# Cross-attention of a decoder layer: the layer-norm root, the output projection and the router's small DVE work put in other places

## The chip, the cores and the metric

The kernel runs on one core of one Trainium2 chip. The metric is the device time of one execution in microseconds; the median of 3 runs of the kernel before is 1839.6 us (1839.06 to 1843.44). TensorE is called PE, VectorE DVE, ScalarE ACT, GpSimd POOL, SyncE SP.

## The reference, cut to what matters

One pre-norm decoder layer on x of shape (8, 224, 512) with a context of (8, 750, 512): self-attention, cross-attention with distance biases, and a mixture of 8 experts of which each token takes 2.

```python
x = x + attn(_layernorm(x))
# cross-attention: 16 heads of 32, 224 queries and 750 keys for each of 8 batches
scores = einsum('bhqd,bhkd->bhqk', q, k) * scale + bias    # bias = -slope[h] * |key - query - (750 - 224)|
out    = einsum('bhqk,bhkd->bhqd', softmax(scores), v) @ Wo + bo
x = x + out
h = _layernorm(x)                                          # (x - m) / sqrt(v + eps)
# router of the mixture
scores = h @ Wr.T + br                                     # 8 experts
idx = top_k(scores + biases_N, 2); val = softmax(scores)[idx]; val = val / val.sum()
# the expert: silu(a) * b, down projection, weighted sum, all in fp32
```

fp32 products are made of high and low parts that are rounded for PE: `w_hi`, `w_lo`, and three matmuls for one product.

## The kernel before, in words

The program is a chain of phases. The change lies in `cross_phase`, which takes from about 720 to 1215 us of the profiled execution. It walks through 32 steps, one for each batch and group of four heads (`GROUPS` = 4 groups make a batch), with a loop over s from -1 to 31. In iteration s, for each of the four heads hh:

- PE makes the transposed scores of step s + 1 (`second_scores`, three banks `a_st_bank`, line 1719) and the plain scores of step s + 2 (`first_scores`, three banks `a_s_bank`, line 1700). The plain scores serve the row maxima alone.
- DVE reduces each plain bank to maxima (`maxima`, line 1959) and so sets it free. PE can be ahead of DVE by the three banks and no more.
- ACT takes the exponential of each transposed bank (`exp`, line 1865) and sets it free.
- POOL adds the exponentials of step s + 1 in pairs (`sums`, lines 1568 and 1572): two additions for each head until step 25, and one after that.

After the four heads PE does `values(s)`: 24 matmuls a head group of probabilities by V (line 1748), the transposition of the row maxima of step s + 2 (`turn_max`, line 1734), and the sums over the keys (line 1758). DVE does `row_maxima(s + 2)` (line 1965), for which `turn_max` waits, and then `normalise(s - 1)`: a reciprocal (line 1972) and a product (line 1976). ACT copies the turned maxima into the query tile (`query_rows`, line 1857), for which the next transposed scores wait. POOL splits the normalised output into high and low part (`split_o`, lines 1579 and 1581), behind its sums.

The order is written out by hand: each engine has its own loop with the same indices, and `note` lists in which order banks are taken. Once every four iterations a batch is finished, and work is inserted between the heads. For batch b:

- iteration 4b + 5: `project_out` (line 1771 to 1773), 12 matmuls for each half of the queries, after heads 1 and 3; it waits for `split_o` of step 4b + 3. DVE adds the residual (line 1985), and at the iteration's end takes the `moments` (lines 1990, 1993). POOL adds the output bias to the next batch's rows (line 1558).
- iteration 4b + 6: ACT takes the root of the variance (`root`, line 1876) before head 1. The square root and the exponential need different function tables, and each change is an ACT_TABLE_LOAD. DVE then makes the normalised rows (`hidden`, lines 1997, 2000), PE turns them after head 3. POOL fetches rows (line 1554).
- iteration 4b + 7: PE makes the router's scores (`route`, line 1812) after head 0.

The router's small DVE work, each instruction waiting for the one before it by `then`: `choose` (top two of two batches, at the end of iterations 11, 19 and 27), `slots` (places of the chosen rows, at the end of 20 and 28), `weights` (at the end of 24 and 29). At iteration 3 ACT makes four `w_hi` (line 1902) and DVE four `w_lo` (line 2090), all ahead of head 0. `GOES` says at which iterations PE makes the ranks (`ranks`) that `slots` reads.

## Time and profile before

| | |
|---|---|
| median of 3 runs | 1839.6 us |
| profiled execution | 1850.8 us, its span 1849.1 us |
| PE busy | 1702.0 us (92%) |
| DVE busy | 1069.2 us (58%) |
| ACT busy | 746.2 us (40%) |
| POOL busy | 757.9 us (41%) |
| mean granted PE clock | 0.962 of full speed |

The profiled execution is 11.2 us above the median. The span is the time from the first to the last instruction. Busy shares are means over phases with different limits. In a timeline, a row gives the start, the duration, the engine, the line, what is written and read, and in brackets how long the engine was idle before, and who released it. Rows of PE overlap, since matmuls are pipelined.

### The profile page before, as it was taken

How to read it: one execution, taken by the hardware profiler on the slowest of the kernel's cores; microseconds unless marked ns; L12 is line 12 of the kernel's file. 1: busy time of each engine (PE TensorE's matmuls, PEld its weight loads, DVE VectorE, ACT ScalarE, POOL GpSimd, SP SyncE). 2: the span in 40 equal slices, each digit the busy share in tenths (PEclk: the TensorE clock that was granted, in tenths of full speed). 3: DMA queues.
4: the chain of work that ended last, by engine and by line, in shares of the span. 5: the costliest groups of instructions: out<-in, count | busy, mean ns of one | idle time of the engine just before them, and what ended most of it. 6: DMA issues, size and time to landing. Idle time of an engine off the chain costs nothing. (4 is left out here: it accounts for less than half of the span.)

```text
span 1849.1 us, 34693 instructions
## 1 busy us (share of the span) xinstructions
PE 1702.0 (92%) x11064; PEld 1367.4 (74%) x11064; DVE 1069.2 (58%) x1893; ACT 746.2 (40%) x1332; POOL 757.9 (41%) x856
## 2 busy tenths in 40 slices
PE   6997999999999987899899898889999999999997
PEld 5885777777777766677777676667778787887775
DVE  5553455555555545777777877574563545436553
ACT  3223343433343333655565555522442424224441
POOL 3000322323322322888778657432451515115541
PEclk9998999999999997899899999879999999999999
DMA  7736566655665745997778677244663737355763
GB/s 227 228 131 174 160 174 177 180 167 167 176 178 157 203 133 129 187 197 162 165 154 173 133 153 183 67 129 123 216 223 114 224 114 232 103 144 192 245 218 91
DMA packets 211744, 309.77 MB, mean 168 GB/s; under 512 B 21728, under 2 KB 151344, under 8 KB 207136
## 3 DMA queue, kind: packets, MB, share of 16 engines
q1 hardware_dynamic: 186656, 223.90, 45.5%
q0 software_dynamic: 15472, 41.14, 10.2%
q10 hardware_dynamic: 9504, 43.26, 6.2%
q8 instruction: 68, 1.11, 0.3%
q14 instruction: 44, 0.36, 0.1%
HBM read 224.56 MB, written 83.66 MB: 167 GB/s over the span
## 5 line engine op out<-in xcount | busy, mean ns | idle before, releaser
L1959 DVE TENSOR_REDUCE a_part_max<-a_s_bank 112x1 f32<-112x500 f32 (+1 forms) x384 | 234.8, 672 | 64.3 <-PE a_s_bank L1700 53.5
L1865 ACT ACTIVATE a_prob<-a_st_bank 125x448 f32<-125x448 f32 x384 | 194.5, 545 | 94.6 <-PE a_st_bank L1719 74.8
L2578 DVE TENSOR_TENSOR e_u_sb<-e_u_bank,e_b_row 128x512 f32<-128x512 f32 x134 | 92.2, 688 | 226.6 <-PE e_u_bank L2343 215.9
L2341 PE MATMUL e_u_bank<-e_w_hi,e_xT_hi 128*128 128x512 f32 x536 | 214.6, 400 | 1.2 <-DVE e_w_lo L2571 0.4
L2343 PE MATMUL e_u_bank<-e_w_hi,e_xT_lo 128*128 128x512 f32 x536 | 211.2, 394 | 0.0
L2342 PE MATMUL e_u_bank<-e_w_lo,e_xT_hi 128*128 128x512 f32 x536 | 210.7, 393 | 0.0
L2501 POOL DMA_INDIRECT out<-l_rows,e_y_row x33 | 53.0, 1605 | 316.6 <-ACT l_rows L2455 163.1
L2402 ACT ACTIVATE e_g_hi<-e_g_bank 128x256 fp32r<-128x256 f32 x133 | 51.2, 385 | 313.2 <-PE e_g_bank L2350 299.0
L1568 POOL TENSOR_TENSOR a_part_sum<-a_prob 125x448 f32<-125x448 f32 x128 | 146.4, 1147 | 66.3 <-ACT a_prob L1865 66.1
L876 POOL TENSOR_TENSOR m_prob_sum<-m_prob 112x224 f32<-112x224 f32 x128 | 85.3, 672 | 170.7 <-ACT m_prob L1084 170.2
L2341 PEld LDWEIGHTS e_u_bank<-e_w_hi,e_xT_hi 128*128 128x128 f32 x536 | 101.8, 190 | 25.4 <-DVE e_xT_lo L2566 3.9
L1572 POOL TENSOR_TENSOR a_part_sum<-a_part_sum,a_prob 125x448 f32<-125x448 f32 x100 | 114.5, 1145 | 14.4
L2343 PEld LDWEIGHTS e_u_bank<-e_w_hi,e_xT_lo 128*128 128x128 f32 x536 | 101.6, 190 | 22.1
L2342 PEld LDWEIGHTS e_u_bank<-e_w_lo,e_xT_hi 128*128 128x128 f32 x536 | 101.8, 190 | 20.6
L2360 PE MATMUL e_y_bank<-e_w_hi,e_g_hi 128*128 128x512 f32 x264 | 115.0, 435 | 0.5 <-POOLq L2508 0.5
L2477 POOL TENSOR_TENSOR e_w_lo<-e_w_raw,e_w_hi 128x1024 fp32r<-128x1024 f32 x28 | 100.8, 3611 | 28.3 <-ACT e_w_hi L2412 28.3
L2361 PE MATMUL e_y_bank<-e_w_lo,e_g_hi 128*128 128x512 f32 x264 | 104.5, 396 | 0.0
L2362 PE MATMUL e_y_bank<-e_w_hi,e_g_lo 128*128 128x512 f32 x264 | 103.9, 394 | 0.0
L1153 DVE SCALAR_TENSOR_TENSOR m_kt_lo<-m_o_bank,m_b_col,m_kt_hi 128x500 fp32r<-128x500 f32 x48 | 35.5, 739 | 106.3 <-ACT m_kt_hi L1093 100.9
L2584 DVE TENSOR_TENSOR e_g_sb<-e_gate,e_u_sb 128x256 f32<-128x256 f32 x134 | 65.2, 487 | 42.5 <-ACT e_gate L2397 32.1
L1084 ACT ACTIVATE m_prob<-m_st_bank 112x448 f32<-112x448 f32 x128 | 67.6, 541 | 51.6 <-PE m_st_bank L1011 51.3
L1167 DVE TENSOR_REDUCE m_row_max<-m_s_bank 112x2 f32<-112x448 f32 x128 | 79.0, 617 | 10.7 <-PE m_s_bank L998 10.7
(388 smaller groups left out, 4381.7 us busy)
## 6 DMA issues: line engine op xcount, KB each, us to landing
e_w_raw<-L_ffn_Wl SPq DMA_DIRECT2D x96, 512.0 KB, 8.0
e_b_row<-L_ffn_bl ACTq DMA_DIRECT2D x33, 1024.0 KB, 6.0
k<-m_kt_hi SPq DMA_DIRECT2D x48, 250.0 KB, 3.2
k<-m_kt_lo SPq DMA_DIRECT2D x48, 250.0 KB, 4.2
m_c_in<-ctx POOLq DMA_DIRECT2D x12, 896.0 KB, 9.6
m_q_st<-q SPq DMA_DIRECT2D x96, 112.0 KB, 3.0
m_k_st<-k SPq DMA_DIRECT2D x96, 112.0 KB, 3.0
v<-m_cv SPq DMA_DIRECT2D x48, 224.0 KB
```

Of the source, the lines that this page charges most:

```text
L1568: pool.tensor_tensor(part_sum[w][:, hh, :, :], prob[w][:, hh, 0:2, :], prob[w][:, hh, 2:4, :], ALU.add).then_inc(sum_done, 1)
L1572: pool.tensor_tensor(part_sum[w][:, hh, :, :], part_sum[w][:, hh, :, :], prob[w][:, hh, 4:6, :], ALU.add).then_inc(sum_done, 1)
L1865: act.activation(prob[s % 2][:, hh, 2 * u:2 * u + 2, :], st_bank[n % SB][0:CR, 0:2 * S].rearrange("p (e q) -> p e q", e=2), ACT.Exp).then_ ...
L1959: dve.tensor_reduce(out, scores, AX.X, ALU.max).then_inc(s_free, 1)
L2341: pe.matmul(out, xT_hi[:, slot, k, :], w_h, start=(k == 0), stop=False)
L2342: pe.matmul(out, xT_hi[:, slot, k, :], w_l, start=False, stop=False)
L2343: last = pe.matmul(out, xT_lo[:, slot, k, :], w_h, start=False, stop=(k == KT - 1))
L2360: pe.matmul(y_bank[slot][:, :], g_hi[:, q % 2, t, :], w2_hi[:, q, t, :], start=first, stop=False)
L2361: pe.matmul(y_bank[slot][:, :], g_hi[:, q % 2, t, :], w2_lo[:, q, t, :], start=False, stop=False)
L2362: last = pe.matmul(y_bank[slot][:, :], g_lo[:, q % 2, t, :], w2_hi[:, q, t, :], start=False, stop=end)
L2477: pool.tensor_tensor(w2_lo[:, q, :, :], w2_raw[:, q, :, :], as_f32(w2_hi[:, q, :, :]), ALU.subtract).then_inc(w2_ready, 1)
L2578: dve.tensor_tensor(u_sb[:, q % 2, :, :], u_bank[q % 2][:, :].rearrange("p (h n) -> p h n", h=2), b1_row[:, slot, :, HC * q:HC * q + HC], ...
```

## The change

1. **Root.** ACT's `root(b)` moves from before head 1 of iteration 4b + 6 to the end of iteration 4b + 5, ahead of `query_rows`. `moments(b)` moves from the end of iteration 4b + 5 to behind its second residual, ahead of head 3's maxima.
2. **Projection.** `project_out` and `residual` come after heads 0 and 2 in place of 1 and 3.
3. **Choices.** `choose` for batches 0 to 3 moves from the ends of iterations 11 and 19 to 13 and 21, in two parts, after heads 0 and 2 (where PE projects). The one at the end of 27 stays.
4. **Places and weights.** The first ranks move from iteration 20 to 21, `slots` is cut in four (after head 3 of 21 and 22, after heads 1 and 3 of 23), `weights` in three (after head 3 of 24, heads 0 and 1 of 25). The second ranks come after head 1 of 28 in place of head 3, with the parts of `slots` after heads 1, 2, 3 and at the end of 28, and those of `weights` after heads 1, 2, 3 of 29. ACT's exponentials of the router go to before head 1 of 24 and before head 0 of 29.
5. **Weight splits.** At iteration 3 one `w_hi` and one `w_lo` stand ahead of each head.

No arithmetic is added or taken away.

```diff
-    GOES = {20: (0, 8), 28: (8, FIRST_TILES)}
+    GOES = {21: (0, 8), 28: (8, FIRST_TILES)}
+    RANKED = {21: 3, 28: 1}
...
-                        if hh % 2 == 1 and batch_at(s, 1) is not None:
+                        if hh % 2 == 0 and batch_at(s, 1) is not None:
                             project_out(batch_at(s, 1), hh // 2)
...
-                        if s in GOES and hh == 3:
+                        if s in GOES and hh == RANKED[s]:
                             ranks(s)
...
-                        if s == 3 and hh == 0:
-                            act.wait_ge(dlo_ready, HEADS // 2)
-                            act.wait_ge(w_loaded, DMA)
-                            for kk in range(KT):
-                                act.activation(w_hi[:, kk, :], w_raw[:, kk, :], ACT.Copy).then_inc(whi_ready, 1)
-                        if hh == 1 and batch_at(s, 2) is not None:
-                            root(batch_at(s, 2))
+                        if s == 3:
+                            if hh == 0:
+                                act.wait_ge(dlo_ready, HEADS // 2)
+                                act.wait_ge(w_loaded, DMA)
+                            act.activation(w_hi[:, hh, :], w_raw[:, hh, :], ACT.Copy).then_inc(whi_ready, 1)
+                        if s == 24 and hh == 1:
+                            score_exp(21)
+                        if s == 29 and hh == 0:
+                            score_exp(28)
...
+                    if batch_at(s, 1) is not None:
+                        root(batch_at(s, 1))
                     if s + 2 < STEPS:
                         query_rows(s + 2)
...
+                        if s in (13, 21) and hh % 2 == 0:
+                            choose((s - 13) // 4, (s - 13) // 4 + 2, hh // 2)
+                        if (s, hh) == (24, 3):
+                            weights(21, 0)
...
+                        if s == 29 and hh:
+                            weights(28, hh - 1)
+                        if hh % 2 == 0 and batch_at(s, 1) is not None:
                             residual(batch_at(s, 1), hh // 2)
+                            if hh == 2:
+                                moments(batch_at(s, 1))
...
+                        if (s, hh) == (21, 3):
+                            slots(21, 0)
...
+                        if s == 28 and hh:
+                            slots(28, hh - 1)
```

ACT in iterations 5 and 6, before (`third` and `a_q_st` are query tiles, `a_std` is the root):

```order
L1857 ACTIVATE third<-a_st_bank 8x896
L1865 ACTIVATE a_prob<-a_st_bank 125x448 x12
L1857 ACTIVATE a_q_st<-a_st_bank 8x896
L1865 ACTIVATE a_prob<-a_st_bank 125x448 x3
L1876 ACT_TABLE_LOAD
L1876 ACTIVATE a_std<-a_mv,a_eps 112x2
L1865 ACT_TABLE_LOAD
L1865 ACTIVATE a_prob<-a_st_bank 125x448 x9
```

And the same place of the changed kernel:

```order
L1858 ACTIVATE third<-a_st_bank 8x896
L1866 ACTIVATE a_prob<-a_st_bank 125x448 x12
L1877 ACT_TABLE_LOAD
L1877 ACTIVATE a_std<-a_mv,a_eps 112x2
L1858 ACTIVATE a_q_st<-a_st_bank 8x896
L1866 ACT_TABLE_LOAD
L1866 ACTIVATE a_prob<-a_st_bank 125x448 x12
```

The root and both table loads now stand around `query_rows` and no longer between exponentials.

PE at the first projection half of iteration 5, before: heads 0 and 1 (their last rows) and the first three of twelve projection matmuls.

```order
L1700 MATMUL a_s_bank<-a_k_st,a_q_st 112x250 x2
L1704 MATMUL a_s_bank<-a_rel_q,a_d_hi 112x224
L1719 MATMUL a_st_bank<-third 125x224 x2
L1700 MATMUL a_s_bank<-a_k_st,a_q_st 112x500
L1719 MATMUL a_st_bank<-third 125x224 x2
L1700 MATMUL a_s_bank<-a_k_st,a_q_st 112x500
L1719 MATMUL a_st_bank<-third 125x224 x2
L1723 MATMUL a_st_bank<-a_rel_k,a_d_hi 125x224
L1700 MATMUL a_s_bank<-a_k_st,a_q_st 112x250 x2
L1704 MATMUL a_s_bank<-a_rel_q,a_d_hi 112x224
L1771 MATMUL a_s_bank<-a_w_hi,a_o_split 112x512
L1772 MATMUL a_s_bank<-a_w_lo,a_o_split 112x512
```

And now, from the end of head 0:

```order
L1701 MATMUL a_s_bank<-a_k_st,a_q_st 112x250 x2
L1705 MATMUL a_s_bank<-a_rel_q,a_d_hi 112x224
L1772 MATMUL a_s_bank<-a_w_hi,a_o_split 112x512
L1773 MATMUL a_s_bank<-a_w_lo,a_o_split 112x512
L1774 MATMUL a_s_bank<-a_w_hi,a_o_split 112x512
```

PE reaches the reading of `a_o_split`, which POOL writes, one head sooner.

DVE at the second half of iteration 13, now (in the order before, the four rows from CAST to `r_before` stood at the end of iteration 11, ahead of head 0, and the BN rows behind the product `a_o_f`):

```order
L2024 CAST a_top_f<-a_top_i 112x32
L2026 TENSOR_TENSOR r_pick<-a_iota_e,a_top_f 112x32 x2
L2028 TENSOR_TENSOR r_mask<-r_pick 112x32
L2030 TENSOR_TENSOR r_before<-r_before,r_mask 112x8 x4
L1992 TENSOR_TENSOR a_x_new<-a_s_bank,a_xh 112x512
L1997 BN_STATS a_bn<-a_x_new 112x6 x2
L2000 BN_AGGR a_mv<-a_bn 112x2 x2
L1966 TENSOR_REDUCE a_part_max<-a_s_bank 112x1 x2
L1966 TENSOR_REDUCE a_part_max<-a_s_bank 112x2
L1972 TENSOR_REDUCE a_row_max<-a_part_max 112x4x2
L1979 RECIPROCAL a_rinv<-a_or_bank 128x224
L1983 TENSOR_TENSOR a_o_f<-a_or_bank,a_rinv 128x224
```

Ahead of the row maxima and of `a_o_f` there now stand the moments, and in 13 and 21 the second part of the choice.

## Rows read from the trace of the kernel before

**Rows 1.** Page, section 1: PE; busy us, share of the span, instructions.

```profile
PE 1702.0 (92%) x11064; PEld 1367.4 (74%) x11064; DVE 1069.2 (58%) x1893; ACT 746.2 (40%) x1332; POOL 757.9 (41%) x856
```

**Rows 2.** Windows between turned maxima: PE, PEld, DVE, ACT, POOL busy; PEclk, DMA, GB/s.

```profile
776.64:1168.33 391.69, 359.89 (x3524) 283.00 (x3520) 303.04 (x576) 214.17 (x386) 284.27 (x279) 0.95 0.75 161
776.64:792.77 16.13, 14.06 (x121) 11.22 (x118) 12.79 (x20) 9.19 (x17) 12.90 (x13) 0.79 1.08 195
...
846.69:857.17 10.48, 10.38 (x120) 8.22 (x116) 9.14 (x16) 7.04 (x13) 9.28 (x11) 1.00 0.88 184
857.17:873.47 16.30, 16.20 (x145) 12.30 (x141) 10.95 (x19) 7.04 (x13) 12.13 (x12) 1.00 0.54 107
...
888.63:900.62 11.99, 11.89 (x136) 9.72 (x133) 8.68 (x15) 7.03 (x13) 9.22 (x10) 1.00 0.82 177
900.62:916.93 16.31, 12.94 (x120) 10.43 (x116) 14.41 (x37) 7.23 (x13) 11.34 (x12) 0.79 0.57 115
...
988.63:1002.25 13.62, 11.32 (x128) 8.95 (x124) 12.30 (x23) 10.57 (x18) 11.30 (x11) 1.00 1.04 232
...
1118.70:1168.33 49.63, 44.98 (x446) 34.18 (x442) 34.87 (x85) 20.57 (x39) 28.84 (x31) 0.97 0.50 135
1168.33:1189.79 21.46, 16.84 (x173) 12.72 (x169) 8.14 (x20) 15.99 (x22) 16.30 (x17) 0.84 0.44 135
```

**Rows 3.** PE's waits from 776.64 to 1189.79: total us, times, longest.

```profile
PE a_st_bank L1719 <- ACT a_prob L1865: 18.4, 10, 2.9
PE a_s_bank L1700 <- DVE a_part_max L1959: 12.8, 8, 3.3
```

**Rows 4.** Timeline of iteration 6 at the root.

```profile
823.05 1.28 ACT L1876 ACT_TABLE_LOAD   x1
...
824.66 1.28 ACT L1865 ACT_TABLE_LOAD   x1
...
826.55 0.48 PE L1719 MATMUL a_st_bank<-a_q_st,a_k_st 104*125 104x224 f32 x2 [2.20 <-ACT a_prob L1865]
```

**Rows 5.** Timeline, tail and head of iteration 5; DVE at its end.

```profile
803.26 0.35 PE L1734 MATMUL a_st_bank<-ident,a_row_max 112*8 112x112 f32 x2
...
806.26 0.27 PE L1704 MATMUL a_s_bank<-a_rel_q,a_d_hi 112*112 112x224 f32 x1
...
817.11 2.48 PE L1748 MATMUL a_or_bank<-a_prob,a_v_sb 125*32 125x224 f32 x48
817.22 0.69 DVE L1985 TENSOR_TENSOR a_x_new<-a_s_bank,a_xh 112x512 f32<-112x512 f32 x1 [1.93 <-PE a_s_bank L1773]
...
819.79 1.28 DVE L1990 BATCH_NORM_STATS2 a_bn<-a_x_new 112x6 f32<-112x512 f32 x2
```

**Rows 6.** Timeline of POOL: ends of two steps in a row, and the bias.

```profile
848.52 0.67 POOL L1581 TENSOR_TENSOR a_o_split<-a_o_f,a_o_split 128x224 fp32r<-128x224 f32 x1
...
859.75 0.67 POOL L1581 TENSOR_TENSOR a_o_split<-a_o_f,a_o_split 128x224 fp32r<-128x224 f32 x1
...
874.96 2.38 POOL L1558 TENSOR_TENSOR a_xh<-a_xh,a_out_bias 112x1024 f32<-112x1024 f32 x1
```

**Rows 7.** Timeline of the choice at the end of iteration 11, and a later one.

```profile
901.35 0.74 DVE L2014 TENSOR_TENSOR a_zb<-r_z,a_c_bias 112x32 f32<-112x32 f32 x1
...
903.22 0.18 DVE L2021 CAST a_top_f<-a_top_i 112x32 f32<-112x32 uint32 x1
...
903.76 1.09 DVE L2025 TENSOR_TENSOR r_mask<-r_pick 112x32 f32<-112x32 f32 x1
...
906.64 3.02 DVE L1959 TENSOR_REDUCE a_part_max<-a_s_bank 112x1 f32<-112x500 f32 x5
907.38 0.76 PE L1700 MATMUL a_s_bank<-third 100*112 100x500 f32 x1 [3.27 <-DVE a_part_max L1959]
...
1135.16 0.19 DVE L2025 TENSOR_TENSOR r_mask<-r_pick 112x32 f32<-112x32 f32 x1
```

**Rows 8.** Timeline of DVE: the weight splits of iteration 3.

```profile
778.70 3.01 DVE L2090 TENSOR_TENSOR a_w_lo<-l_rows,a_w_hi 128x512 fp32r<-128x512 f32 x4 [1.52 <-ACT a_w_hi L1902]
```

More of the change, by code:

```diff
@@ L2006, in scores_done, with choose, best @@
                                       r_bias[:, :].unsqueeze(1).broadcast_to([QR, 2, EXPERTS]), ALU.add).then_inc(s_free, 1)
-                def choose(b0, b1):
+                def choose(b0, b1, part=None):
                     t0, n = 2 * b0, 2 * (b1 - b0)
+                    tiles = slice(t0, t0 + n)
+                    TE = [QR, n, EXPERTS]
+                    if part in (None, 0):
+                        best(t0, n, b1)
+                    if part == 0:
+                        return
+                    then(dve.tensor_copy(top_f[:, 0:n, :], top_i[:, 0:n, :]))
+                    for j in range(2):
+                        last = dve.tensor_tensor(pick[j][:, tiles, :], iota_e[:, 0:n, :], top_f[:, 0:n, j].unsqueeze(2).broadcast_to(TE), ALU.is_equal)
+                    then(last)
+                    then(dve.tensor_tensor(mask[:, tiles, :], pick[0][:, tiles, :], pick[1][:, tiles, :], ALU.add))
+                    for t in range(t0, t0 + n):
+                        then(dve.tensor_tensor(before[:, t + 1, :], before[:, t, :], mask[:, t, :], ALU.add))
+                    dve.sem_inc(chosen, 1)
+                def best(t0, n, b1):
                     tiles = slice(t0, t0 + n)
@@ L2020, in choose, with slots @@
                     then(last)
-                    then(dve.tensor_copy(top_f[:, 0:n, :], top_i[:, 0:n, :]))
-                    for j in range(2):
-                        last = dve.tensor_tensor(pick[j][:, tiles, :], iota_e[:, 0:n, :], top_f[:, 0:n, j].unsqueeze(2).broadcast_to(TE), ALU.is_equal)
-                    then(last)
-                    then(dve.tensor_tensor(mask[:, tiles, :], pick[0][:, tiles, :], pick[1][:, tiles, :], ALU.add))
-                    for t in range(t0, t0 + n):
-                        then(dve.tensor_tensor(before[:, t + 1, :], before[:, t, :], mask[:, t, :], ALU.add))
-                    dve.sem_inc(chosen, 1)
-                def slots(s):
+                def slots(s, part):
                     t0, t1 = GOES[s]
@@ L2041, in slots @@
-                    dve.tensor_tensor(row[:, 0:n, :], bank[0:QR, 0:n * EXPERTS].rearrange("p (t e) -> p t e", e=EXPERTS),
-                                      places["first_slot"][:, :].unsqueeze(1).broadcast_to(TE), ALU.add).then_inc(s_free, 1)
-                    dve.wait_ge(s_free, at + 1)
-                    for j in range(2):
-                        then(dve.tensor_tensor(prod[:, 0:n, :], row[:, 0:n, :], pick[j][:, t0:t1, :], ALU.mult))
-                        then(dve.tensor_reduce(slot_f[:, j, 0:n], prod[:, 0:n, :], AX.X, ALU.add))
@@ L2060, in weights @@
+                def weights(s, part):
                     t0, t1 = GOES[s]
```

117 lines of the change are left out of this document (65 added, 52 removed).

## The prediction, written before the changed kernel was run

> **What bounds the kernel now.** I read the busy times first: PE is busy for 92% of the span [rows 1], so only what PE waits for, and the clock it runs at, can be won. Then I cut the phase that changes into iterations, from one turned maximum to the next [rows 2]. Without anything odd there are four kinds, and a batch takes one of each: a plain iteration takes 10.48 us (846.69:857.17), one with the projection 16.30, one with the turning of the hidden rows 13.62 less a wait of 2.20, so 11.4, and one with the router's scores 11.99. In the first, second and fourth the granted clock is 1.00 and PE is busy for all but 0.1 us. Iterations 3 to 29 are 8 plain ones (3 counted so), 7, 6 and 6: 83.8 + 114.1 + 68.5 + 71.9 = 338.3 us. They take 391.7 [rows 2]. The excess of 53.4 us is what this change can reach, and 2.9 us or a bit more in iteration 30.
>
> The excess is of two sorts. PE's waits [rows 3]: 18.4 us on the exponentials, of which 2.9 lie in iteration 30, and 12.8 on DVE's maxima, 28.3 in the window. And the clock: 0.95 over the window, 5% of 391.7 = 19.6 us. Together 48; the rest is small stretching. After some waits PE runs at 1.2 GHz for a while: iteration 12 waits 3.27 us [rows 7] and is 5.8 us over plain at a clock of 0.79; iteration 18 waits 2.2 us, its clock stays 1.00, and it loses no more than the wait [rows 2].
>
> **The root.** In iteration 6 ACT loads a table (1.28 us), takes the root, loads the other (1.28 us), and PE stands for 2.20 us [rows 4], since exponentials do not free their banks. There are seven such roots, six in the window and one in iteration 30. Moved to the end of iteration 4b + 5, the root lies beside `values`. Count from P, the end of the second projection half (817.11, rows 5). PE does head 3, about 1.66 us (plain iteration 10.48, less 3.1 to the end of head 0 and 2.4 for the values part, over three heads), then 2.4 us of values (817.11 to 819.52, rows 2 and 5), and turns the maxima at T = P + 4.1. ACT's last exponential ends near P + 2.2, the load and the root at P + 3.8, so `query_rows`, which waits for T, is not held. The second load ends at about T + 2.6 and the first exponential at T + 3.15, where PE wants its bank at T + 3.1. I take 0.2 us of wait in each: 1.2 us left in six iterations instead of 13.2.
>
> The page on ScalarE in the Trainium skill (ScalarE: Activation LUTs, What ACT_TABLE_LOAD costs) puts a switch at 1283 ns and a drain of 1380 ns more. In these rows nothing of 1380 ns stands behind a load: 823.05 and 824.66 are 1.61 us apart, load and root together. By the page the first exponential would come some 1.4 us later and PE would wait 1.6 rather than 0.2 us, ten us over seven batches.
>
> **The moments ahead of head 3.** They must be there, or the root would wait. From P DVE now does the residual (0.6 us net of overlap), the moments (1.28 us, rows 5, and 0.2 for the aggregates), three maxima (3.02 for five, so 1.8, rows 7) and the row maxima (0.1): it ends at P + 4.1 to 4.5. PE wants them at P + 4.1. So a wait of 0 to 0.6, taken 0.4, seven times: 2.8 us. What is late next is the normalisation, which stood in front of the moments and takes 1.9 us (817.91 to 819.79, rows 5). It now ends at T + 1.9, where it ended at T + 0.3.
>
> **The projection a head sooner.** PE reaches the end of head 0 at T + 3.1 (803.26 to 806.26 and one more tenth, rows 5), and then needs `split_o` of the step before last. POOL finishes that at 860.42 in iteration 9, which is T + 3.25 from 857.17 [rows 2, 6]. Before, PE came 1.7 us later and never waited. With the stretch before it unchanged the wait would be 0.15 us. But POOL is short of slack: two split ends in a row are 11.23 us apart [rows 6], more than a plain iteration of PE. The chain since the last projection: normalisation 1.9, split 1.1, bias 2.4 (874.96), then three steps of about 10.9 (11.23 less a short pause for the first exponential, my choice), and 0.7 for issuing a load: T + 38.8 to the end of the split. PE needs 11.6 + 12.0 + 10.5 + 3.1 = 37.2. So a wait of 1.6 us; its bounds are 0.15 and, with 11.23 three times, 2.6. It comes in iterations 5, 9, 13, 17, 21: 8.0 us. From step 25 on POOL does half the sums, and there is none. This is a wait that the roots' standstill paid for until now.
>
> **The choices.** At the ends of 11 and 19, DVE is away from 901.35 to 906.64 while PE fills three banks and stops for 3.27 us [rows 7]; iteration 12 costs 5.8 us too much, and so does 20, of the same shape. Put beside the projection, part one takes 1.87 us (901.35 to 903.22) and DVE is idle there for about 1.9 [rows 5]: nothing. Part two takes 3.42 (903.22 to 906.64), 1.5 more than its cover, and what follows it is the residual and the row maxima: 1.5 us each, 3.0 in all, bounds 0 and 3.4 each.
>
> The page on SBUF (SBUF — State Buffer, Who interferes with whom) says that a DVE instruction with two SBUF inputs and a GpSimd one that reads SBUF hold each other off whole. The rows agree: the same sum of two 112x32 tiles took 1.09 us at 903.76 and 0.19 at 1135.16 [rows 7]. It speaks against pieces: each may have to wait once more for a POOL addition. Twelve pieces at 0.9 us would be 11 us more, if none had cover.
>
> **Places, weights, splits.** The first `slots` and `weights` leave a wait behind today and are cut; after it I keep 1.5 us for all pieces in 22 to 25 (a piece of 1.0 to 1.4 us against a lead of PE of two banks, 1.1 us), and 0.6 for the ranks' matmuls. At iteration 3 (16.13 us, clock 0.79) ACT and DVE split weights ahead of the first head; DVE's 3.01 us for four [rows 8] do not get shorter, and twelve maxima at 0.6 with four splits at 0.75 make 10.2 us for four heads where PE needs 6.6. With PE's lead taken off, about 2.3 of the 5.65 us stay.
>
> For 27 to 29 little moves: they take 49.63 us against 11.99 + 10.48 + 16.30 = 38.8, so 10.8 over, and the choice at the end of 27 and the places of 28 are the same DVE work in a row. The three parts of `weights` now stand inside 29, where maxima are still due; before, they were behind them. I add 1.6 us.
>
> **The sum.** Left in the window after the change: 2.3 (splits) + 8.0 (POOL) + 2.8 (row maxima) + 1.2 (exponentials) + 3.0 (choices) + 1.5 + 0.6 + 10.8 + 1.6 = 31.8. From 53.4 that is 21.6 us won. Iteration 30 has its wait of 2.9 us and a clock of 0.84 over 21.46 us [rows 2]; I take 2.9 and 1.4 of clock: 25.9. New waits of 1.5 us can drop the clock as the old ones did. Of about five in the bounds of the two cases above (2.5 us and nothing) I charge 1.2 each: 6.0. Won: 19.9 us. Nothing behind the phase changes: the loads for the experts are issued by PE's progress, and DMA's share is 0.44 over iteration 30. The profiled execution took 1850.8 us, so 1831; the median, 11.2 below it, goes from 1839.6 to 1820.
>
> **Rivals.**
> 1. POOL keeps up and DVE's moments fit: no 8.0, no 2.8, no 6.0 of clock. Then 36.7 us are won: 1803. For it: the wait of 0.15 that the rows of iteration 9 give. Against: 11.23 us a step. Chance 0.19.
> 2. The pieces stall: each is held by POOL, 11 us more as worked out, and 0.4 us more on each row maximum. Won 6 to 8: 1832. For it: 1.09 against 0.19. Against: the projection's cover. Chance 0.15.
> 3. The root is not hidden, because a switch costs more than its load (the drain above, which no row shows): 1.4 us more in seven batches: 1830. Chance 0.03.
> 4. Slower. Each projection iteration now has two new waits, on POOL's split and on the row maxima, fourteen in all. If the clock falls at each as it did after the waits of iteration 3, which lost 0.21 of 16.13 = 3.4 us, that is 48 us against the 25.9 won: 1862. The point from which it decides is eight falls. For it: in most old places a wait of 2.2 us or more did it. Against: 0.4 to 1.6 us is shorter, and 18 had none at 2.2. Chance 0.04.
> 5. It does not reach the end: the phase ends on a chain that does not shorten, such as POOL's table entries and their load, or the waits just move. 1838 to 1840. Against: PE is the engine that all wait for there. Chance 0.05.
>
> The forecast has 0.54, with a range of its own from 1811 to 1829. The range for 8 in 10, over the first three: 1806 to 1834. What a measurement can tell from no change is 0.3%, 5.5 us, so 1834.1 and 1845.1. Faster: 0.53 + 0.19 + 0.11 + 0.02 = 0.85; slower 0.04 from case 4 and 0.01 as a rest; within 0.3% 0.10.
>
> **What would show it.** In the changed profile: the iterations 4b + 6 at 11.4 to 11.8 us with no wait on `a_prob` of 2.2 (else the root is not hidden); plain iterations 12 and 20 at 10.5; waits of PE on `a_o_split` of about 1.6 us at lines of the projection in five iterations (none: rival 1); waits at the turned maxima of some 0.4; iteration 3 near 12.8; the clock over the window at 0.97 to 0.98, not 0.95. The mean clock at 0.92 or waits on `a_part_max` above 12.8 us would make the prediction wrong.

## The result, and the profile after

On the chip of the result the changed kernel takes 1847.0 us (median of 20 runs, 1840.95 to 1850.39), the kernel before 1840.0 (20 runs, 1835.57 to 1845.83): ratio 1.0034, 95% interval [1.0024, 1.0044]. It is slower by a third of a per cent. The forecast of 1820 and its range were wrong, and so was the sign.

The profiled execution of the changed kernel took 1846.5 us, its span 1844.8, at a mean clock of 0.967. That is 4.3 us *less* than the profiled execution of before, although the medians say 7 us more: the execution of before took 11 us more than its median, and more than any of the 20 runs (1845.83 at most). One pair of profiles is therefore no measure of the change. What it shows is where the time lies. First the page's busy times of the changed kernel, in the columns of [rows 1]:

```profile
PE 1698.4 (92%) x11064; PEld 1359.8 (74%) x11064; DVE 1074.9 (58%) x1893; ACT 745.3 (40%) x1332; POOL 760.3 (41%) x856
```

The same instruction counts on every engine. Then the windows of the changed kernel, in the columns of [rows 2]: the whole window from iteration 3 to 29, and iterations 3, 5, 6, 12, 13 and 23.

```profile
777.11:1169.11 392.00, 360.50 (x3524) 279.09 (x3521) 313.27 (x589) 215.53 (x389) 286.00 (x279) 0.96 0.76 162
777.11:790.22 13.11, 11.49 (x120) 8.61 (x116) 11.50 (x20) 9.03 (x17) 12.43 (x12) 1.00 1.10 197
800.71:819.74 19.03, 16.40 (x145) 12.50 (x142) 11.08 (x22) 8.62 (x15) 14.91 (x15) 1.00 1.02 213
819.74:833.58 13.84, 11.74 (x125) 9.14 (x125) 12.88 (x20) 9.01 (x16) 11.44 (x10) 1.00 1.00 203
...
900.30:910.81 10.51, 10.41 (x120) 8.24 (x117) 9.10 (x16) 7.03 (x13) 9.31 (x11) 1.00 0.90 186
910.81:928.76 17.95, 16.70 (x144) 12.57 (x141) 15.21 (x43) 8.61 (x15) 12.12 (x12) 1.00 0.58 124
...
1059.10:1075.50 16.40, 13.90 (x136) 10.55 (x133) 13.89 (x26) 7.13 (x13) 10.71 (x11) 0.90 0.63 136
```

The window is as long as before, 392.0 against 391.7. By kinds of iteration (the predicted column is the terms of the prediction, without its 6.0 us for the clock):

| iterations | before | predicted | after |
|---|---|---|---|
| 3 (weight splits) | 16.1 | 12.8 | 13.1 |
| 5, 9, 13, 17, 21 (projection) | 84.6 | 95.1 | 93.2 |
| 6, 10, 14, 18, 22, 26 (root, hidden rows) | 88.4 | 69.6 | 88.9 |
| 12 and 20 | 32.5 | 21.0 | 21.0 |
| 23 and 25 | 30.5 | 28.7, +1.5 for all pieces | 34.7 |
| 27 to 29 | 49.6 | 51.6 | 51.3 |
| the other eight | 89.9 | 89.9 | 89.9 |

Five rows of seven came within 2 us, two of them (the projection and 27 to 29) for other reasons than were given, as the section on the prediction shows. One did not move at all where 19 us were to be won, and that of 23 and 25 is 4.5 us above its term. PE's waits of the changed kernel from 777.11 to 1189.79 (the end that the rows of before have), in the columns of [rows 3], tell what took their place:

```profile
PE a_s_bank L1701 <- DVE a_part_max L1966: 12.3, 10, 2.4
PE a_st_bank L1720 <- ACT a_prob L1866: 4.5, 7, 1.3
PE a_s_bank L1772 <- DVE a_part_max L1966: 3.5, 2, 1.9
PE a_st_bank L1735 <- DVE a_row_max L1972: 2.6, 6, 1.0
PE a_or_bank L1759 <- POOL a_part_sum L1569: 2.6, 1, 2.6
PE a_s_bank L1772 <- POOL a_o_split L1582: 2.2, 1, 2.2
PE a_s_bank L1701 <- DVE a_row L2058: 2.0, 1, 2.0
PE a_s_bank L1785 <- DVE a_part_max L1966: 1.6, 1, 1.6
```

The wait on the exponentials fell from 18.4 to 4.5 us, as it should. The one on the maxima stayed at 12.3, although the two choices of 3.3 us left it, and six other rows appeared.

**The root's iteration.** The answer to [rows 4], the timeline of iteration 10 of the changed kernel, where the table load, the exponentials and DVE's hidden rows stand:

```profile
874.79 1.28 ACT L1866 ACT_TABLE_LOAD   x1 [0.61 <-PE a_st_bank L1720]
...
876.09 4.88 ACT L1866 ACTIVATE a_prob<-a_st_bank 125x448 f32<-125x448 f32 x10
...
876.69 0.48 PE L1720 MATMUL a_st_bank<-a_q_st,a_k_st 104*125 104x224 f32 x2 [0.54 <-ACT a_prob L1866]
```

```profile
877.44 1.85 DVE L1966 TENSOR_REDUCE a_part_max<-a_s_bank 112x1 f32<-112x500 f32 x3 [0.57 <-PE a_s_bank L1701]
879.20 0.15 DVE L2004 RECIPROCAL a_rstd<-a_std 112x2 f32<-112x2 f32 x1
879.39 1.83 DVE L2007 TENSOR_SCALAR l_rows<-a_x_new,a_mv,a_rstd 112x512 f32<-112x512 f32 x2
881.14 2.42 DVE L1966 TENSOR_REDUCE a_part_max<-a_s_bank 112x1 f32<-112x500 f32 x4
...
881.86 0.48 PE L1701 MATMUL a_s_bank<-first 100*112 100x500 f32 x1 [1.46 <-DVE a_part_max L1966]
```

The 2.20 us on `a_prob` are gone, and two waits stand there: 0.54 us behind the load of the exponential's table, which starts only with the first scores (874.79) and not right behind the copy of the query rows; and 1.46 us on the maxima, because DVE spends 879.20 to 881.22 on `hidden` while PE fills its three banks. Before, the same work lay inside the standstill: it was over at 880.46, and PE, which waited for the exponentials, went on at 880.50. It was also shorter. The two rows in iteration 10 of before, and then those in iteration 26 of the changed kernel, where POOL has no addition beside them:

```profile
879.32 1.14 DVE L2000 TENSOR_SCALAR l_rows<-a_x_new,a_mv,a_rstd 112x512 f32<-112x512 f32 x2
```

```profile
1111.34 1.00 DVE L2007 TENSOR_SCALAR l_rows<-a_x_new,a_mv,a_rstd 112x512 f32<-112x512 f32 x2
```

In 6, 10, 14, 18 and 22 of the changed kernel the second row takes 1.37 us, beside POOL's additions, in place of 0.54, and PE waits 1.46 or 1.47; in 26 it waits 0.64. About half of the wait is thus DVE's work and the other half what that work gains in length beside POOL. The split is read from one iteration without additions; no run isolates it.

2.0 us of wait stand in place of 2.2, and the clock falls in four of the six iterations (0.88 or 0.89), where it fell in three before (0.89, 0.89 and 0.79).

**The projection.** The answer to [rows 5, 6], timeline of iteration 5: POOL's split and the projection's first matmul.

```profile
805.52 0.66 POOL L1582 TENSOR_TENSOR a_o_split<-a_o_f,a_o_split 128x224 fp32r<-128x224 f32 x1
...
806.23 0.49 PE L1772 MATMUL a_s_bank<-a_w_hi,a_o_split 128*112 128x512 f32 x1 [2.25 <-POOL a_o_split L1582]
```

The wait on the split came, but only here. In 9, 13, 17 and 21 there is none: the prediction had given POOL's chain iterations 4b + 6 of 11.6 us, and they still take 13.6 to 15.5. At 5 there is no projection ahead, so that chain does not exist there. What changed ahead of it is iteration 3, three us shorter, and the wait goes with that in the runs below: with the projection in its old place it is none where 3 takes 16.1 us (the kernel before) and 0.68 at 13.1 (e2_small_work), and a head sooner it is 1.13 at 14.6 (e1_root_side) and 2.25 at 13.1. The cost of a head sooner lies elsewhere: in 13 and 21 DVE makes the second part of the choice, the residual and the moments in a row (15.21 us busy of 17.95), and PE waits 0.67 on `a_x_new`, 0.48 on the row maxima, and at 21 another 1.6 for the ranks.

**Pieces.** The answer to [rows 7]: DVE and then POOL in iteration 23, part three of `slots`.

```profile
1066.21 0.25 DVE L2066 CAST a_slot_n<-a_slot_f 112x16 int32<-112x16 f32 x1
1066.50 0.17 DVE L2067 TENSOR_SCALAR a_spot_n<-a_slot_n 112x16 int32<-112x16 int32 x1
1066.71 1.04 DVE L2068 CAST a_spot_f<-a_spot_n 112x16 f32<-112x16 int32 x1
1067.78 1.05 DVE L2069 SCALAR_TENSOR_TENSOR a_lane_f<-a_spot_f,a_slot_f 112x16 f32<-112x16 f32 x1
1068.86 0.17 DVE L2070 SCALAR_TENSOR_TENSOR a_place_f<-a_lane_f,a_spot_f 112x16 f32<-112x16 f32 x1
```

```profile
1066.57 1.14 POOL L1573 TENSOR_TENSOR a_part_sum<-a_part_sum,a_prob 125x448 f32<-125x448 f32 x1
1067.67 1.13 POOL L1569 TENSOR_TENSOR a_part_sum<-a_prob 125x448 f32<-125x448 f32 x1
```

Five instructions of 0.2 us take 2.8: one ends where POOL's addition ends (1067.7), the next where the following one does (1068.8). PE then waits 2.40 us at 1069.80, and the clock falls to 0.90 in this iteration, which had neither before. In iteration 28 it is larger still, DVE first and POOL behind it:

```profile
1137.89 2.78 DVE L2057 SCALAR_TENSOR_TENSOR r_before<-a_pad,r_before 1x1 f32<-1x1 f32 x1
```

```profile
1137.33 3.32 POOL L1569 TENSOR_TENSOR a_part_sum<-a_prob 125x448 f32<-125x448 f32 x3
```

An instruction on one element takes 2.78 us beside three sums of POOL in a row, and PE waits 2.04 us for the row behind it. The Trainium skill says (SBUF — State Buffer, Who interferes with whom) that a DVE instruction with two SBUF inputs contends with a GpSimd one that reads SBUF. The row agrees, with its end at 1140.67 beside that of the sums at 1140.65; that several of POOL's go first is what it adds.

### The profile page after: what moved, and what is told of

Same layout as the page of the kernel before. It is cut to its first block and busy times, and to the rows that moved or that the text cites. A ratio compares the mean times of both kernels' runs of the same rounds, so it can differ in the third digit from the quotient of the medians.

```text
span 1844.8 us, 34701 instructions
## 1 busy us (share of the span) xinstructions
PE 1698.4 (92%) x11064; PEld 1359.8 (74%) x11064; DVE 1074.9 (58%) x1893; ACT 745.3 (40%) x1332; POOL 760.3 (41%) x856
## 5 line engine op out<-in xcount | busy, mean ns | idle before, releaser
L2621 DVE TENSOR_TENSOR e_g_sb<-e_gate,e_u_sb 128x256 f32<-128x256 f32 x134 | 65.2, 486 | 42.5 <-ACT e_gate L2434 32.5
L1084 ACT ACTIVATE m_prob<-m_st_bank 112x448 f32<-112x448 f32 x128 | 67.6, 541 | 51.5 <-PE m_st_bank L1011 51.3
L1749 PE MATMUL a_or_bank<-a_prob,a_v_sb 125*32 125x224 f32 x1536 | 85.5, 374 | 0.0
```

## The experiments

There are fourteen results, of nine altered kernels and of the changed one, from four chips (A to D); on each the kernel before ran too. Ratios are to that, with 95% intervals. Only the changed kernel and three of the others ran on two chips, so a small difference between two chips proves nothing. "Window" is the stretch from iteration 3 to 29 in the profiled execution.

| chip (before) | kernel | median us | ratio | window |
|---|---|---|---|---|
| A (1852.1) | e1_root_side | 1852.6 | 1.0001 [0.9977, 1.0025] | 390.3 |
| A | e2_small_work | 1844.8 | 0.9961 [0.9938, 0.9984] | 388.3 |
| A | e3_choices | 1845.1 | 0.9971 [0.9946, 0.9995] | 392.3 |
| A | e4_hidden_act | 1841.6 | 0.9942 [0.9915, 0.9968] | 391.2 |
| B (1840.1) | a2_changed_again | 1845.2 | 1.0026 [1.0011, 1.0042] | 392.0 |
| B | e6_heads_1_3 | 1834.6 | 0.9957 [0.9938, 0.9975] | 383.7 |
| B | e7_act_early | 1831.5 | 0.9928 [0.9902, 0.9955] | 378.9 |
| B | e5_all_cover | 1818.8 | 0.9876 [0.9853, 0.9898] | 359.8 |
| C (1852.2) | e8_early_1_3 | 1824.4 | 0.9839 [0.9806, 0.9872] | 368.5 |
| C | e9_root_act | 1839.6 | 0.9926 [0.9899, 0.9953] | 382.3 |
| D (1854.8) | a3_changed_third | 1850.9 | 0.9981 [0.9962, 1.0000] | 394.4 |
| D | e1_again | 1856.2 | 1.0004 [0.9983, 1.0025] | 400.4 |
| D | e2_again | 1845.1 | 0.9944 [0.9924, 0.9964] | 388.0 |
| D | e5_again | 1828.6 | 0.9860 [0.9837, 0.9883] | 368.4 |

**The two halves (e1_root_side, e2_small_work).** Parts 1 and 2 of the change alone, and the changed kernel with them put back (the projection, and with it the choices, behind heads 1 and 3).

```diff
 e1 = before with
-                        if hh == 1 and batch_at(s, 2) is not None:
-                            root(batch_at(s, 2))
+                    if batch_at(s, 1) is not None:
+                        root(batch_at(s, 1))
...
-                        if hh % 2 == 1 and batch_at(s, 1) is not None:
+                        if hh % 2 == 0 and batch_at(s, 1) is not None:
                             residual(batch_at(s, 1), hh // 2)
+                            if hh == 2:
+                                moments(batch_at(s, 1))
 e2 = the changed kernel with these lines the other way round
```

> The kernel before with only the root, the moments and the projection moved as in the change; choices, places, weights and splits stay where they were. Theory (the wait only moved: with ACT's root gone, DVE's hidden rows in head 1 of iterations 4b + 6 hold the maxima, and PE waits for those): iterations 4b + 6 keep about 2 us of PE waits, 0.5 on a_prob and 1.5 on a_part_max, the projection iterations get 0.5 to 2 us longer, and the time is 0.0 to 0.4% above the kernel before. Rival (the forecast's term was right, and it is the small pieces that cost): iterations 4b + 6 near 11.6 us and the time 0.5 to 1.0% below the kernel before.

> The changed kernel with root, moments and projection put back as before; choices, places, weights and splits stay in pieces. Theory (the pieces that stand in the projection's cover pay, those of iterations 21 to 23 and 28 cost the same again): iterations 12 and 20 at 10.5 us, 13 and 21 longer than before by 1 to 4 us, 23 and 28 longer by 2 to 4; the time within 0.3% of the kernel before. Rival (pieces are the whole loss): 0.3 to 0.6% above it. Forecast's terms: 0.6% below.

Moving the root, the moments and the projection gives nothing, here and on chip D. All that the change wins is won by the small work: choices, pieces and splits.

**The choices alone (e3_choices).** The kernel before with `choose` in two parts behind heads 1 and 3 of 13 and 21, where PE projects. With it the first ranks and `slots`, whole, go from 20 to 21, which the cut does not show.

```diff
+                        if s in (13, 21) and hh % 2 == 1:
+                            choose((s - 13) // 4, (s - 13) // 4 + 2, hh // 2)
...
-                        if b == 1:
-                            dve.wait_ge(const_ready, 1)
-                        choose(b - 1, b + 1)
+                    if s == 27:
+                        choose(4, 6)
```

> The kernel before with only the choices of batches 0 to 3 moved to iterations 13 and 21, in two parts beside the projection halves (after heads 1 and 3), and ranks and places of the first half one iteration later, whole. Theory (DVE idles 2 us beside each projection half): iterations 12 and 20 fall from 16.3 to 10.5 us, 13 and 21 grow by 1.5 to 2.5 each; 6 to 8 us faster, 0.3 to 0.45%. Rival (DVE work costs PE the same wherever it stands in this phase): no change within 0.1%.

Iterations 12 and 20 take 10.51 us and 13 takes 16.38 (16.32 before): with the projection behind heads 1 and 3 the second part costs nothing at 13, where the prediction had 1.5 us. At 21 the ranks wait 1.06 us for it. Where the moments stand in front of the row maxima too (e5, e6, e8), 13 takes 17.45 us. The whole window of e3 is nevertheless 392.3: the whole `slots` at the end of 21 makes PE wait 4.44 us in 22 (18.77 us at a clock of 0.82), and the clock fell to 0.72 to 0.80 in 26 to 28. By the ratio the choices are worth 0.3%, beside 0.4 to 0.6% for all the small work; the intervals overlap.

**The hidden rows on ACT (e4_hidden_act, e7_act_early).** The changed kernel, with the two 112x512 rows of `hidden` made by ACT behind heads 1 and 2 as `x * rstd - m * rstd`; DVE makes only the reciprocal and a 112x2 product, in e4 behind head 0 of iteration 4b + 6, in e7 at the end of 4b + 5.

```diff
-                    for t in range(2):
-                        dve.tensor_scalar(xh[b % 2][:, t, :], x_new[:, t, :], mv[:, t, 0:1], rstd[:, t:t + 1], ALU.subtract, ALU.mult).then_inc(h_ready, 1)
+                    dve.scalar_tensor_tensor(nmr[:, :], mv[:, :, 0], -1.0, rstd[:, :], ALU.mult, ALU.mult).then_inc(rstd_done, 1)
...
+                        if hh in (1, 2) and batch_at(s, 2) is not None:
+                            hidden_act(batch_at(s, 2), hh - 1)
...
-                        if hh == 1 and batch_at(s, 2) is not None:
-                            hidden(batch_at(s, 2))
+                    if batch_at(s, 1) is not None:          # e7; e4: hh == 0 and batch_at(s, 2)
+                        hidden(batch_at(s, 1))
```

> The changed kernel with the hidden rows of each batch (two 112x512 products) made by ACT after heads 1 and 2 of iterations 4b + 6 and no longer by DVE in head 1; DVE keeps the reciprocal and one 112x2 product. Theory (DVE's hidden rows are what PE waits for there now): the wait of 1.47 us on a_part_max in those iterations goes, they take 12.0 to 12.8 us instead of 13.6 to 15.5, and the time falls by 10 to 18 us against the changed kernel, 0.5 to 1.0%, so below the kernel before. Rival (the clock and POOL set these iterations): they stay at 13.6 to 15.5 us, the time within 0.2% of the changed kernel.

e4 shortened iterations 14, 22 and 26 to 12.5 to 13.1 us, but 6, 10 and 18 took 16.5, 15.2 and 16.5, with waits of 1.8. What tells them apart is the 112x2 product. Here it is in iteration 18, DVE first and POOL behind it:

```profile
989.11 0.15 DVE L2015 RECIPROCAL a_rstd<-a_std 112x2 f32<-112x2 f32 x1
989.30 2.36 DVE L2017 SCALAR_TENSOR_TENSOR a_nmr<-a_mv,a_rstd 112x2 f32<-112x2 f32 x1
```

```profile
988.17 2.38 POOL L1560 TENSOR_TENSOR a_xh<-a_xh,a_out_bias 112x1024 f32<-112x1024 f32 x1
990.50 1.14 POOL L1570 TENSOR_TENSOR a_part_sum<-a_prob 125x448 f32<-125x448 f32 x1
```

It ends when the second of POOL's two additions ends. In 6, 10, 14, 18, 22 and 26 it takes 2.36, 2.37, 1.64, 2.36, 0.16 and 0.68 us. e7 moves only it and the reciprocal.

> Like the kernel with ACT making the hidden rows, but DVE's reciprocal and 112x2 product stand right behind the normalisation at the end of iteration 4b + 5 and no longer after head 0, where the product took 2.36 us beside POOL's bias sum. Theory (it is POOL's hold on small DVE instructions with two inputs that PE waits for, not their work): the wait of 1.28 us on a_part_max in iterations 4b + 6 goes, they take 11.8 to 12.2 us; 5 to 12 us faster than that kernel, 1.0 to 1.3% faster than before. Rival (DVE lags from the normalisation anyhow): a wait of 1 us or more stays, time within 0.2%.

The timeline of e7 at the head of iteration 10, DVE, ACT and PE:

```profile
874.07 0.15 DVE L2015 RECIPROCAL a_rstd<-a_std 112x2 f32<-112x2 f32 x1
...
874.22 1.28 ACT L1867 ACT_TABLE_LOAD   x1 [0.61 <-PE a_st_bank L1721]
874.25 0.34 DVE L2017 SCALAR_TENSOR_TENSOR a_nmr<-a_mv,a_rstd 112x2 f32<-112x2 f32 x1
874.52 1.83 DVE L1976 TENSOR_REDUCE a_part_max<-a_s_bank 112x1 f32<-112x500 f32 x3
...
876.12 0.48 PE L1721 MATMUL a_st_bank<-a_q_st,a_k_st 104*125 104x224 f32 x2 [0.53 <-ACT a_prob L1867]
```

And its windows, the whole one and iteration 10, in the columns of [rows 2]:

```profile
776.34:1155.19 378.85, 354.13 (x3525) 274.66 (x3522) 302.93 (x583) 220.07 (x401) 284.15 (x279) 0.97 0.79 169
872.32:884.82 12.50, 11.60 (x125) 9.03 (x126) 11.36 (x19) 9.78 (x18) 10.10 (x9) 1.00 0.90 199
```

Iterations 6, 10, 14 and 18 take 12.50 us each at a clock of 1.00, where the changed kernel takes 13.8 to 15.4. Beside the changed kernel on the same chip e7 is 13.6 us faster at the median and 13.1 in the window, and those 13.1 are the difference of the six iterations alone (88.9 to 75.8). This shows that the missing cover of the hidden rows was what cost the root's gain. The 0.8 us of wait that stay are on `a_prob`, behind the table load.

**The projection back behind heads 1 and 3 (a2_changed_again, e6_heads_1_3).** e6 is the changed kernel with `project_out`, `residual`, `moments` and the choices a head later; a2 the changed kernel itself on that chip.

```diff
-                        if hh % 2 == 0 and batch_at(s, 1) is not None:
+                        if hh % 2 == 1 and batch_at(s, 1) is not None:
                             residual(batch_at(s, 1), hh // 2)
-                            if hh == 2:
+                            if hh == 3:
                                 moments(batch_at(s, 1))
```

> The changed kernel once more, beside the three others and the kernel before on one chip. Theory (waits moved, none gone for good): 0.0 to 0.4% slower than before. Rival (the first comparison was of a pair of executions with few clock falls before and many after): faster by 0.2 to 0.6%, as the two parts measured alone would give together (1.0001 and 0.9961).

> The changed kernel with the projection back behind heads 1 and 3; moments behind the second residual, now after head 3, the choices beside the halves. Theory (the head sooner is what makes PE wait for POOL's split in iteration 5, for the residual in 13 and 21 and for the row maxima in all seven): these waits go, iterations 5, 9, 13, 17 at 16.3 to 16.6 us, not 16.8 to 19.0; iterations 4b + 6 unchanged near 15; 4 to 8 us (0.2 to 0.4%) faster than the changed kernel. Rival (the row maxima then come later and hold PE more): the same time or slower.

e6 is 10.5 us below the changed kernel at the median and 8.3 in the window. Iterations 5, 9, 13, 17 and 21 take 85.4 us against 93.2; the wait on the split in 5 goes from 2.25 to 0.68. The root does not need the head: it is as well hidden in e6 (0.53 us a time, as in the changed kernel). So the second part of the change bought nothing; beside the rest it cost some 10 us.

**The root's part alone, repaired (e9_root_act), and both repairs (e8_early_1_3).** e9 is the kernel before with the root at the end of 4b + 5, moments behind the second residual at head 3, and the hidden rows as in e7; e8 is the changed kernel with the edits of e6 and e7.

> The kernel before with the root's part alone, repaired: root at the end of iteration 4b+5, moments behind the second residual at head 3, ACT makes the hidden rows, DVE's reciprocal and 112x2 product at the end of 4b+5. Projection, choices, places, weights and splits stay as before. It tests whether the root was the right place and only the cover of the hidden rows was missing. Theory: iterations 6, 10, 14, 18, 22 and 26 take 12.5 us (26 about 13.1) instead of 15.2, 15.2, 16.6, 13.6, 13.6 and 14.2 us; with iteration 30 some 12 us less than the profiled execution of before, 8 to 12 us of the median: ratio 0.994 to 0.996. Rival: what the standstill of the root gave POOL and DVE is missed elsewhere (split late at the projection, choices), the wait only moves and the ratio is 0.998 to 1.002, as when the root's side was moved without the repair.

> The changed kernel with both repairs at once: ACT makes the hidden rows and DVE's reciprocal and 112x2 product stand at the end of iteration 4b+5, and the projection is back behind heads 1 and 3. The places and weights stay in pieces. If the two repairs add up: iterations 4b+6 take 12.5 us each, 5 takes 17.2, 9 and 17 16.4, 21 18.2, and 23, 28 and 29 keep the length that the pieces give them (about 16.4, 17.5 and 19.5), so about 371 us for iterations 3 to 29 and a ratio near 0.991, with the last 0.4% of the kernel with everything under cover owed to the pieces at 23, 28 and 29. Rival: all of the gain over each single repair comes from their combination, pieces or not, and the ratio is 0.987 to 0.988, as in that kernel. Second rival: with shorter iterations 4b+6 and the projection later POOL's split or the choice comes late, and the ratio stays at 0.993 to 0.996, as with one repair.

e9's window:

```profile
777.09:1159.34 382.25, 359.31 (x3524) 280.48 (x3520) 298.47 (x573) 219.98 (x400) 283.11 (x279) 0.96 0.77 164
```

Iterations 6, 10, 14 and 18 take 12.49 or 12.50, and nothing is given back at 5, 9, 13 and 17 (16.35 to 16.39). Of the rest 12 and 20, the choices, wait 3.68 instead of 3.27, and 25 takes 19.9 us at a clock of 0.91 where it took 18.5. The root's part, which gives nothing as it was written, gives 0.74% with cover. One caution: e1 had the projection a head sooner and e9 has not, so the two differ in more than the cover. The root moved without cover and with the projection in its old place is e6, and it is no faster than e2, the small work without the root (0.9957 and 0.9961, on two chips); e7 changes the cover alone. e8 adds the repairs up: 368.5 in the window, 0.9839. That is better than the 0.991 expected and on its chip no worse than e5 on the others, so the extra worth of whole pieces is not shown by a time; the windows show that 23 and 25 together take 33.7 us in e8 and 30.3 in both runs of e5.

**Everything under cover (e5_all_cover).** e8 with the later parts of `slots` and `weights` moved: `slots` behind head 3 of 21 to 24, `weights` behind heads 1 and 3 of 25, the second `slots` and `weights` whole at the ends of 28 and 29. The second ranks are back behind head 3 of 28, and the router's exponentials go to 25 and to the end of 29.

```diff
-                        if s == 23 and hh % 2 == 1:
-                            slots(21, 2 + hh // 2)
-                        if s == 28 and hh:
-                            slots(28, hh - 1)
+                        if (s, hh) == (23, 3):
+                            slots(21, 2)
+                        if (s, hh) == (24, 3):
+                            slots(21, 3)
...
+                    if s == 28:
+                        for part in range(4):
+                            slots(28, part)
+                    if s == 29:
+                        for part in range(3):
+                            weights(28, part)
```

> All together: ACT makes the hidden rows with the small products early, projection after heads 1 and 3, choices beside it, places of the first half after head 3 of 21 to 24, weights beside the projection of 25, the second places and weights whole at the ends of 28 and 29. Theory: iterations 4b + 6 at 12, 5 to 21 at 16.3 to 17, 12 and 20 at 10.5, 23 at 12; 25 to 32 us faster than before, 1.4 to 1.7%. Rival (POOL's chain of sums then sets the pace): no more than 15 us, 0.8%, with waits of PE on a_o_split.

Windows of e5: the whole one, and iterations 23, 28 and 29.

```profile
778.11:1137.92 359.81, 344.90 (x3525) 268.99 (x3521) 297.21 (x573) 219.50 (x400) 283.67 (x279) 1.00 0.84 175
1040.42:1054.32 13.90, 11.97 (x133) 9.73 (x133) 12.25 (x22) 7.02 (x13) 12.37 (x13) 1.00 0.96 199
1106.86:1119.78 12.92, 12.43 (x143) 9.67 (x139) 12.36 (x39) 7.15 (x13) 9.66 (x11) 1.00 0.72 224
1119.78:1137.92 18.14, 17.50 (x161) 13.00 (x157) 13.50 (x37) 8.49 (x15) 9.39 (x10) 1.00 0.33 107
```

The window is 32 us shorter and the clock stays at 1.00. Beside a2, the changed kernel on this chip, it is 32.2 us less in the window and 26.4 at the median. In these two traces 5.8 us are lost ahead of iteration 3, where the kernels are the same, and 3.0 behind 29, where PE now waits 5.75 us for the last batch's rows from ACT (1174.87), against 4.20 from DVE in the changed kernel on the chip of the result and 5.49 on D. It beats both kernels, on both chips where it ran.

**All of it on one chip (second set).** The kernels are those above.

> The changed kernel again, together with its two halves. On two chips it was 0.3% slower than before, where before takes 1840 us; on two other chips before takes 1852 us. If the difference between chips lies in how often the clock falls in the old waits, the changed kernel (fewer of them) is level or faster where before takes 1852: ratio 0.996 to 0.999. If it is a property of the chip that hits every kernel alike, it is 1.002 to 1.004 on each.

> The kernel before with root, moments and projection moved alone, beside the whole change on one chip. If the two halves add up, the whole is this ratio times that of the other half. If the halves hinder each other (choices now in front of head 3's row maxima and of the projection's maxima: waits of 1.15 and 2.27 us in iterations 13 and 21 against 0.29 and 2.0), the whole is 0.2 to 0.4% above the product.

> The changed kernel with root, moments and projection put back, beside the whole change on one chip. By the windows it is 388.3 us against 392.0 for the whole change: 0.2% faster than the whole. Rival: the root's side is worth what its removed waits suggest, and the whole is faster than this half.

> The kernel with everything under cover, for the size of its gain beside the changed kernel on one chip: by the windows 32 us shorter than the changed kernel between iterations 3 and 29, at the median 26 to 28 us less. If the order of chips matters it is 1.2% faster than before where before takes 1840 us and 1.8% where it takes 1852.

Two things are learned. The halves seem to hinder each other: 1.0004 times 0.9944 is 0.9948, the whole is 0.9981, 0.3% above, which is about as much as the three intervals together leave open. In the traces iteration 13 waits 1.15 us in the whole, 0.30 with the root's side alone and none with the small work alone. And the size of the result depends on the chip: 1.0034 and 1.0026, slower beyond the interval, where before takes 1840 us, and 0.9981 [0.9962, 1.0000], level or faster, where it takes 1855. In the three traces of the changed kernel the iterations up to 24 that run at full clock have the same length to 0.05 us (9 is 16.83 or 16.84). Where they differ in this phase is how often the clock falls, but most of the 9.8 us between the traces of the changed kernel from the chip of the result and from D lies elsewhere: 2.4 us in the window and 8.0 behind iteration 29, where the clock is 0.981 on the one and 0.968 on the other. In iteration 14 a wait of 2.00 us costs 15.26 us at 0.89 on the chip of the result and 13.83 at 1.00 on D. In e5's last run PE waited 1.84 us at the end of 23, and iteration 24 behind it took 13.49 us at 0.75:

```profile
1054.33 0.35 PE L1736 MATMUL a_st_bank<-ident,a_row_max 112*8 112x112 f32 x2 [1.84 <-DVE a_row_max L1982]
```

In e5's first run the same wait, 1.83 us, left 24 at 10.51 us and a clock of 1.00.

## Why the prediction was wrong

**The failed step is the root term.** The prediction took "0.2 us of wait in each" of the iterations 4b + 6, because it followed only ACT's chain. It listed DVE's work in iteration 4b + 5 one by one, but never priced `hidden` in 4b + 6, which did not move. It cost nothing before since the root's standstill of PE hid it; without that, 2 us of DVE between maxima, against a lead of three banks, cost 1.46, about half of it the second row's 1.37 us beside POOL. With the table load's 0.54 the wait is 2.0 in place of 0.2 and the clock falls at least as often as it did: 19.3 us over the table's row. e7, e8 and e9 take DVE's rows away and the iterations fall to 12.50. The 13.1 us that e7 wins in the window are most of the 15.9 by which it missed (392.0 for 376.1).

**The table load.** Taken: the second load ends at T + 2.6 and the exponential barely comes late. In iteration 10 (T = 872.89) it ends at T + 3.2, since it starts with the first scores instead of behind `query_rows`, and PE waits 0.54 us a time. The drain of 1380 ns of rival 3 is not to be seen: the load ends at 876.07 and the exponentials start at 876.09. The rival's arithmetic (1.4 us a batch more) has about the size of the wait on the maxima, by chance; its mechanism is not what happened.

**POOL's split.** 1.6 us five times was predicted, 2.25 once was found. The chain was computed against iterations 4b + 6 of 11.6 us, which did not come about, and for iteration 5, the only one that waited, it does not exist. But e7, with 12.5 in those iterations and the projection behind head 0, shows no wait on the split at 9 either, so the term was too large also on its own ground. Its sum, 95.1 for five projections, was near the 93.2 measured by luck in part: 8.0 us of split were 2.25, and in 21 a wait of 1.6 for the ranks and a clock of 0.85 filled up what was missing.

**The moments ahead of head 3.** 0.4 us each: 0.28 to 0.30 in 5, 9, 17 and 25, more where the choice stands ahead. Right.

**The choices.** 12 and 20 at 10.5, as written; 1.5 us for the second part at 13 and 21 were right in size with the head sooner (0.67 on the residual and 0.2 more on the row maxima at 13, 0.67 and the ranks' 1.6 at 21); with heads 1 and 3 the part costs nothing at 13 and 1.06 at 21 (e3).

**The pieces.** 1.5 us for 22 to 25 was too little: 23 alone costs 4.4 and 25 another 1.6. Rival 2, each piece held by POOL, is what the rows of 23 and 28 show. It was the right mechanism with the wrong weight. Splits at iteration 3 (13.1 for 12.8) were right. 27 to 29 came out (51.3 for 51.6) by luck: 29, where the addition was made, did not grow (21.7 for 21.6), 28 grew by 2.8 us with its pieces, and 27 shrank by 1.3.

**The clock.** Six us for new falls was charged, and the window's clock came out at 0.96, not 0.97 to 0.98. The prediction said that a clock of 0.92 or waits on `a_part_max` above 12.8 would show it wrong; they were 0.96 and 12.3 + 3.5 + 1.6 us. The second one did. Rival 5, with a chance of 0.05, names what happened ("the waits just move"), though at 1838 to 1840. Rival 4, slower by falls of the clock in the projection iterations, is not it: in the trace of the result the clock fell in one of these, 21.

**The base.** The sum was made against one execution 11 us above the median, and its whole excess of 53.4 us was taken as there to win in the median too. Execution against execution the forecast was 1831 and 1846.5 was measured: 15.5 us missing, about the window's 15.9 (392.0 for 376.1). Iteration 30 gave most of its 4.3 us: from its start to the turning of the last batch's hidden rows it is 33.3 us in place of 36.7, although a wait of 2.56 on POOL's last sum stands there in place of half of the one on the exponentials. The other 11 of the 27 us between forecast and result come from the base. Where in the program the median execution of before is 11 us shorter than the traced one is not known: before was traced only once. The runs on D, where before takes about what that execution took, give 0.9981: the change is worth half a per cent more there than on the chip of the result.

## What to carry to other kernels

A stall that is taken away has been hiding work on every engine, not only on the one that stalled: before pricing it at nothing, list what each engine did during it, also the work that the change does not touch, and ask where PE's lead of banks covers it. Small DVE work goes where PE reads something else for two us (the projection here), and not beside POOL's additions. When gains hang on the clock, take lengths of iterations at full clock from the traces and the verdict from many runs, on more than one chip.

## What the runs showed of the hardware

- The table for a function is loaded when the next ACTIVATE's own wait is over. In the changed kernel the load starts at 874.79 us, 0.61 us after ACT went idle, by its releaser. ACT has nothing to do in that gap, but the load is not put there. PE's wait of 0.52 to 0.54 us behind it is shorter than this gap; that an earlier load would take it away is argued, not shown.
- A DVE instruction of 1x1 took 2.78 us beside POOL's sums, one of 112x2 2.36 beside the bias, a CAST of 112x16, which has one input only, 1.04 beside one of the sums, and a TENSOR_SCALAR of 112x512, with one large input, 1.37. Elsewhere the same 1x1 instruction took 0.36 (before, 1146.86), the 112x2 product 0.16 in iteration 22 of e4 and 0.34 in seven of eight batches of e7, the CAST 0.17 (before, 1032.49) and the TENSOR_SCALAR 0.54.
- The clock after the same wait is not the same from one execution to the next: after 2.0 us of wait the iteration had 0.89 or 1.00. A fall to 0.89 costs 1.4 to 1.6 us in an iteration of 14, one to 0.79 2.9 us (iteration 6 against 10 of e2). On one chip the kernel before spreads over 9 to 21 us, and over the 35 runs on A the time falls by 1.7 us for 0.001 of mean clock. Between chips, with medians of 1840, 1840, 1852, 1852 and 1855 us, the clock explains only a part: B's is 0.0018 above A's, 3 of the 12 us by that rate (an estimate); the rest was not traced.
